# Moving the start of the split U tiles within 128 bytes of memory, step by step and stream by stream

## The reference

```
L0: xw = h @ W1.T;  m = Be * (H.T @ xw);  out = Dn * (H @ m) + b      (twice, hidden width 512)
L1: agg = norm(adj) @ (h @ W);  out = tanh(agg + b)
L2: out = A @ x @ w,  A = exp(leaky(8 tanh(s/8))) * adj^T rescaled by row sums
L3: three times adj @ (x @ W) + b, relu between them
```

## Time and profile before

| | |
|---|---|
| median of 3 runs | 1412.08 us (1411.73 to 1412.53) |
| the profiled execution | 1411.93 us |
| its span, first to last instruction | 1410.1 us |
| PE busy | 1373.2 us, 97% |
| PEld busy | 1324.9 us, 94% |
| DVE, ACT, POOL busy | 87%, 70%, 71% |
| chain that ended last | 95% PE |
| granted TensorE clock, mean | 0.995 |

### The profile page before, as it was taken

The page is one execution under the profiler, slowest core; times in us unless marked ns, Lnnn a source line. Parts: engine busy times, 40 slices in busy tenths (PEclk is TensorE's granted clock), DMA queues, the critical chain, the costliest instruction groups (busy, mean ns, idle before and its releaser), DMA issues.

```text
span 1410.1 us, 34586 instructions
## 1 busy us (share of the span) xinstructions
PE 1373.2 (97%) x10900; PEld 1324.9 (94%) x10900; DVE 1227.0 (87%) x3873; ACT 981.3 (70%) x2312; POOL 997.7 (71%) x2005
## 2 busy tenths in 40 slices
PE   4899999999999999999999999999999999999997
PEld 3799999999999999999999999999999999999996
DVE  5788898898898898898898898898898898898884
ACT  3577777777776777777776777776777777777763
POOL 3677777777777777777777777777777777777751
PEclk8999999999999999999999999999999999999999
DMA  6011121111111111111111111111111111111100
GB/s 190 2 42 36 46 52 34 44 52 34 45 52 34 45 52 34 45 52 33 45 52 32 46 52 31 47 52 31 47 52 30 48 52 29 49 52 31 33 20 23
DMA packets 83079, 62.70 MB, mean 44 GB/s; under 512 B 40304, under 2 KB 65520, under 8 KB 83056
## 3 DMA queue, kind: packets, MB, share of 16 engines
q1 hardware_dynamic: 83056, 62.43, 16.2%
HBM read 45.62 MB, written 16.78 MB: 44 GB/s over the span
## 4 chain that ended last, share of the span: by engine, by line
PE 95%; DVE 2%; POOL 1%; ACT 1%; issue 0%; DMA 0%; SPq 0%; DVEq 0%; POOLq 0%
PE BANK L366 29%; PE BANK L331 24%; PE BANK L373 15%; PE WIDE L366 8%; PE WIDE L342 8%; PE WIDE L373 4%; PE BANK L358 2%; PE BANK L316 2%; PE BANK L385 2%; DMA W<-in_w1t 0%; PE WIDE L279 0%; DVE BN_A L551 0%; POOL LN_A L730 0%; DVE WLO1W L501 0%; DVE BN_C L551 0%
## 5 line engine op out<-in xcount | busy, mean ns | idle before, releaser
L445 ACT ACTIVATE UHI_B<-BANK 128x512 fp32r<-128x512 f32 x96 | 57.2, 596 | 44.8 <-PE BANK L331 44.8
L592 DVE TENSOR_TENSOR ULO_D<-BANK,UHI_D 128x512 fp32r<-128x512 f32 x96 | 66.0, 687 | 24.3 <-ACT UHI_D L445 23.6
L445 ACT ACTIVATE UHI_C<-BANK 128x512 fp32r<-128x512 f32 x96 | 57.2, 596 | 42.1 <-PE BANK L331 42.1
L445 ACT ACTIVATE UHI_D<-BANK 128x512 fp32r<-128x512 f32 x96 | 57.2, 596 | 40.9 <-PE BANK L331 40.9
L445 ACT ACTIVATE UHI_A<-BANK 128x512 fp32r<-128x512 f32 x96 | 57.2, 596 | 40.2 <-PE BANK L331 40.2
L592 DVE TENSOR_TENSOR ULO_C<-BANK,UHI_C 128x512 fp32r<-128x512 f32 x96 | 65.9, 687 | 19.4 <-ACT UHI_C L445 18.7
L592 DVE TENSOR_TENSOR ULO_A<-BANK,UHI_A 128x512 fp32r<-128x512 f32 x96 | 66.0, 687 | 16.1 <-ACT UHI_A L445 15.7
L592 DVE TENSOR_TENSOR ULO_B<-BANK,UHI_B 128x512 fp32r<-128x512 f32 x96 | 65.9, 687 | 14.6 <-ACT UHI_B L445 13.9
L480 ACT ACTIVATE BANK<-BANK 128x256 f32<-128x256 f32 x64 | 23.6, 368 | 63.5 <-DVE BANK L648 63.5
L726 POOL TENSOR_TENSOR LN_D<-MV_D,EPS 128x2 f32<-128x2 f32 x80 | 15.6, 195 | 63.7 <-DVE MV_D L559 63.7
L726 POOL TENSOR_TENSOR LN_A<-MV_A,EPS 128x2 f32<-128x2 f32 x80 | 15.7, 196 | 60.4 <-DVE MV_A L559 60.4
(11 more groups left out here) (501 smaller groups left out, 5940.7 us busy)
## 6 DMA issues: line engine op xcount, KB each, us to landing
X_A<-in_xs SPq DMA_DIRECT2D x16, 256.0 KB, 2.9
X_B<-in_xs SPq DMA_DIRECT2D x16, 256.0 KB, 2.8
X_C<-in_xs SPq DMA_DIRECT2D x16, 256.0 KB, 2.8
X_D<-in_xs SPq DMA_DIRECT2D x16, 256.0 KB, 2.9
out_rows<-O_A SPq DMA_DIRECT2D x16, 256.0 KB, 2.0
out_rows<-O_B SPq DMA_DIRECT2D x16, 256.0 KB, 2.1
out_rows<-O_C SPq DMA_DIRECT2D x16, 256.0 KB, 2.1
out_rows<-O_D SPq DMA_DIRECT2D x16, 256.0 KB, 2.1
```

Of the source, the lines that this page charges most:

```text
L445: nc.scalar.activation(UHI[s][:, 0:J * D], bank(s, step)[:, :], ACT.Copy).then_inc(sem(f"c{step}"), 1)
L592: nc.vector.tensor_tensor(ULO[s][:, 0:J * D], bank(s, step)[:, :], UHI[s][:, 0:J * D].bitcast(F32), ALU.subtract).then_inc(sem(f"l{step}"), 1)
```

## The change

UHI and ULO get 32 more elements (128 bytes) of room each, and a function `u_part` gives the part that a step uses: it begins at element (STARTS + 16) mod 32 of the tile, with one number in STARTS for each pair of steps and stream. Every writer and reader of a step uses the same part: the ACT copy, the DVE subtraction and the matmuls. Since the tiles begin at byte 64, which is 16 elements, the part begins at element STARTS of the 32 that make 128 bytes: at 0 for 0W in all streams, and for 1W to 6W at 24 different places. The number, order, shape and waits of the instructions stay as they are, and tiles behind U move by a multiple of 128 bytes.

```diff
-        UHI = per_stream("UHI", J * DH, dt=F32R)
-        ULO = per_stream("ULO", J * DH, dt=F32R)
+        UHI_ALL = per_stream("UHI", J * DH + 32, dt=F32R)
+        ULO_ALL = per_stream("ULO", J * DH + 32, dt=F32R)
+
+        STARTS = {"0": (0, 0, 0, 0), "1": (6, 18, 20, 26), "2": (4, 22, 30, 13), "3": (2, 10, 24, 12), "4": (8, 14, 17, 28),
+                  "5": (1, 19, 9, 16), "6": (3, 5, 23, 31)}
+
+        def u_part(tiles, step, s):
+            at = (STARTS[step[0]][STREAMS.index(s)] + 16) % 32
+            return tiles[s][:, at:at + J * DH]
...
-                                nc.tensor.matmul(dst, UHI[s][:, at[m]:at[m] + P], w[:, m, :],
+                                nc.tensor.matmul(dst, u_part(UHI_ALL, step, s)[:, at[m]:at[m] + P], w[:, m, :],
...
-                            last = nc.tensor.matmul(dst, ULO[s][:, at[m]:at[m] + P], hi[:, m, :], start=False,
+                            last = nc.tensor.matmul(dst, u_part(ULO_ALL, step, s)[:, at[m]:at[m] + P], hi[:, m, :], start=False,
...
-                    nc.scalar.activation(UHI[s][:, 0:J * D], bank(s, step)[:, :], ACT.Copy).then_inc(sem(f"c{step}"), 1)
+                    nc.scalar.activation(u_part(UHI_ALL, step, s)[:, 0:J * D], bank(s, step)[:, :], ACT.Copy).then_inc(sem(f"c{step}"), 1)
...
-                    nc.vector.tensor_tensor(ULO[s][:, 0:J * D], bank(s, step)[:, :], UHI[s][:, 0:J * D].bitcast(F32),
+                    nc.vector.tensor_tensor(u_part(ULO_ALL, step, s)[:, 0:J * D], bank(s, step)[:, :], u_part(UHI_ALL, step, s)[:, 0:J * D].bitcast(F32),
                                             ALU.subtract).then_inc(sem(f"l{step}"), 1)
```

More of the change, by code:

```diff
@@ L450, in take_hidden @@
                     act.wait_ge(sem("p1U"), c["v"][j])
-                    nc.scalar.activation(UHI[s][:, j * DH:(j + 1) * DH], bank(s, "1U")[:, j, :], ACT.Copy).then_inc(sem("c1U"), 1)
+                    nc.scalar.activation(u_part(UHI_ALL, "1U", s)[:, j * DH:(j + 1) * DH], bank(s, "1U")[:, j, :], ACT.Copy).then_inc(sem("c1U"), 1)
             def hidden_relu(s, c, k):
@@ L599, in low_hidden @@
                     half = slice(j * DH, (j + 1) * DH)
-                    nc.vector.tensor_tensor(ULO[s][:, half], bank(s, "1U")[:, j, :], UHI[s][:, half].bitcast(F32),
+                    nc.vector.tensor_tensor(u_part(ULO_ALL, "1U", s)[:, half], bank(s, "1U")[:, j, :], u_part(UHI_ALL, "1U", s)[:, half].bitcast(F32),
                                             ALU.subtract).then_inc(sem("l1U"), 1)
```

## The result

| | before | after |
|---|---|---|
| median of 5 runs each | 1412.13 us (1411.73 to 1412.53) | 1419.66 us (1419.28 to 1419.67) |
| span of the profiled execution | 1410.1 us | 1417.9 us |

The change costs 7.5 us: the ratio is 1.0052, with a 95% interval of 1.0041 to 1.0063. Forecast were 1406 us; the time lies inside of the range, on the other side of no change. Later kernels ran on several chips, where the kernel before has medians of 1412.1 to 1413.7 us, so the ratio given with each is to the kernel before on its own chip. One execution of e4_place22_everywhere took 1720.67 us at a mean granted clock of 0.752, where its others have 0.994 to 0.996, and is left out.

The account below looks back on a forecast made before the run. PE, busy for 1373.2 of 1410.1 us, was taken to set the pace. The sum 1411.93 - 3.7 (256-column matmuls) - 2.3 (0W) = 1405.9 gave a forecast of 1406 us, range 1391 to 1421.

Parts of the forecast that it names:

- What bounds the kernel: Whole kernel: PE's pace sets the end; DVE, next, has 8.8 us to spare per pass, so PE's savings come out in full.
- Two rhythms of weight load and moving stream: F32R matmuls on PE: weight load and moving stream meet in memory in one of two rhythms, 4.5 ns apart.
- (a): 256-column matmuls of 1W to 6W: half of 52 long turn short, half of 26 short turn long; 3.7 us less.
- (b): 0W, U moved from byte 64 to byte 0: 3 ns per matmul, 2.3 us less; sign: below 394 in all streams.
- (c): The two bias matmuls: only the load beside them changes; 0.4 us at most either way, taken as nothing.
- (d): ACT copy and DVE subtraction at other places: no price, staying near 596 and 687 ns; any cost hidden.
- (e): U steps: untouched and indifferent to the moving operand's place, 275 ns with G at byte 0, 274 at byte 32.
- Rival 1: U's place in all steps: the place does nothing; 1412.1 us, chance 0.20.
- Rival 2: All moved steps: the table hits the short pace everywhere, 20.0 us less, 1392 us; chance 0.11.
- Rival 3: Weight loads of unaligned U cover 33 stretches of 16 bytes, not 32; short steps turn long, 1420 us; chance 0.29.
- The third level: Durations by tile of 256-column matmuls: a level below 276 or above 281 ns would make the forecast wrong; no price given.
- the forecast's own range: Whole kernel: 1399 to 1410 us, with (a) between 0 and 8 and (b) between 0 and 4.6.

Follow-up runs that it names:

- e4_place22_everywhere: U at element 22 of 32 relative to the weights in every step and stream, tiles 4096 bytes apart; 1405.2 us, ratio 0.9939 to the kernel before.
- e7: The change done for 0W alone, all other U at byte 64 with the room of the change; 1412.08 us, ratio 0.9993 to the kernel before.
- p2_kinds: Kernel before plus 18 PE-only series at places 16, 22, 0: unchanged 117.8, 114.5, 118.6 ns; stationary operand repeated 113.5, moving repeated 111.7.
- e2: U at place 0 relative to the weights in every step and stream, tiles 4096 bytes apart; 1421.2 us, ratio 1.0054 to the kernel before.
- p1_all_places: Kernel before plus PE-only series of 16 F32R matmuls at each of 32 places of U; 1529.4 us; only places 10, 19, 22 settle at 113 to 114 ns.
- e1: Changed kernel with U kept at byte 64 everywhere, leaving only the 128 bytes of room; 1412.45 us, ratio 0.9991 to the kernel before.
- p4: Kernel before plus 16 PE-only series, places 16 and 22 moved on by 0 to 7 times 128 bytes; place 22: 113.7 or 113.8 ns at even multiples, 120.0 at odd.

## Why the prediction was wrong, point by point

- **What bounds the kernel** was right for a loss: PE has no idle time after either, and the 123 ns of "all", 64 times, are 7.9 us of the span's 7.8. For a gain it was wrong. "No wait in the middle of the run is left that could grow" rested on busy shares, and 2U's wait for H grew by up to 54 ns as soon as the W steps before it got short (e7: all of a gain of 3.2 us; e4: 20 of 130 ns). The prediction had no term for that wait.
- **Two rhythms of weight load and moving stream** was right as a mechanism (p2_kinds: without one of the two walks, no effect of the place), but the number two was not. The series and e2 show cycles with means of 116.7, 117.8, 118.7 and 120.0 ns, and after has distances up to 126. And the rhythm hangs on the relative address modulo 256 bytes, where the prediction and the change reckoned modulo 128.
- **(a) failed, in the even draw, and with it the sign of the forecast.** I let half of the 26 short matmuls turn long and half of the 52 long ones short. In fact nearly all of the 26 turned long: the share near 113 fell from 0.29 to 0.03, and 2W, 3W and 4W lost 121 ns for each stream and pass, where all 26 x 4.5 = 117 would be the whole. Of the 52 nearly none turned short: 1W, 5W and 6W lost 19 ns. Of the rows of WHI1W, WHI5W and WHI6W, for some of which 276 was the sign, none has a median below 279. The draw isn't even, since 113 is there at 3 of 32 places (p1_all_places), and all three stand in the table for stream B, whose tiles the room moves by an odd multiple of 128 bytes, where none of them is short. Two levels at one place were no reason to take each for as likely at another. The term's upper end of +7.5 us was passed: (121 + 19) x 64 = 9.0, the excess being levels above 118, which the 1 us that I had added for them in the range did not quite cover.
- **(b) was right in sign and near in size:** 0W won 26 ns for each stream and pass, 1.7 us against 2.3. 15 of the 26 came with the room alone, however (e1: 2835), so the place itself gave 11 to 13 ns (after and e7 against e1). The sign that was named for it, below 394 in all four streams, came in part: stream C has medians of 395 and 396.
- **(c) was right:** BIAS4W has 392 ns for 388 and takes 6 ns more of PE's time, 6 x 64 = 0.4 us.
- **(d) was right:** 597 and 686 ns. **(e)** the U steps keep their time in after (2U 891 for 889); in kernels with shorter W steps 2U doesn't, by its wait.
- **Rival 1** (nothing) falls: kernels with the same instructions lie between 1405 and 1421 us.
- **Rival 2** had the possible gain right in its direction, but place 22, at 0.65 near 113, brings 7 us by the ledger (113 x 64 = 7.2) and not 20.
- **Rival 3** gave 1420 and the kernel has 1419.7, yet for the wrong reason. The amount followed from "all 26 fall", which is nearly true (7.7 us for 7.5); that it let 0W gain nothing (1.7 us) and 1W, 5W and 6W lose nothing (1.2 us) cancelled by luck. The cause, one stretch of 16 bytes more, is refuted by place 0 (aligned, 1421.2 us) and place 22 (not aligned, 1405.2 us). The rule of the Trainium skill that stood beside it ("SBUF — State Buffer", Specifications) finds no sign here of a price for the crossing.
- **Not seen at all** was that the 128 bytes of room shift the tiles. I took "a multiple of 128 bytes" for no change. It is worth nothing in sum (e1), but 6 ns for a matmul at place 22 (p4), and it took away the three short places of the table.
- **The third level**, named as what would make the forecast wrong, appeared.
- **A slip in the sums:** the forecast's own range was put at 1399 to 1410 us. With its terms, (a) between 0 and 8 and (b) between 0 and 4.6, it reaches up to 1412.

What stays open: the rule that leads from relative address and moment of entry to a rhythm. I can measure which places have the short one; why 10, 19 and 22, and 13 moved on by 128 bytes, have it wasn't found, nor what in the entry lets 16 settle at 113 in one setting and at 118 in another. Open is as well what sets the moment at which H is ready for 2U: the chain through DVE, POOL and ACT wasn't taken apart.

## What to carry to other kernels

Where PE is never idle and its matmuls are about as long as the load of the next weights, the relative address of the two operands (modulo 256 bytes at least) is a tuning knob of some per cent for each matmul. Don't draw it at random or vary it step by step: measure the places in a series behind the work, take one that settles short after most of what can go ahead (place 22 did after seven of eight), use it for all steps, and check the levels by tile in the whole kernel, since gains of single steps don't add. Where PE has no idle time, look too at how far ahead of each PE step its input is ready: that slack, here nearly 60 ns at 2U, bounds what a faster PE gives, and no busy share shows it. And a tile that grows moves all those behind it; keep such room at multiples of 256 bytes or more if levels are to be compared.

## What the runs showed of the hardware

An F32R matmul of 256 columns behind another starts 111.7 ns later if its moving operand is one repeated element, 113.5 ns later if the stationary one is, and 113 to 123 ns later on average, mostly in repeating cycles, if both walk through memory (113.3 at place 22; 122 at place 27 in p1, 123.3 in 5W of stream B of after). Which of these it is hangs on the relative address of the two modulo 256 bytes and on what ran before. The same cycle of five distances (115, 117, 122, 120, 119) came back for operands both at byte 0, both at byte 64, in the kernel and in the series behind it. With 512 columns the distance is 232 to 233 ns in the series, so the effect of the three places is below 1 ns there on average; in the kernels 0W takes 2822 to 2856 ns, 2.8 ns for a matmul from end to end. With 128 columns it is 111.7 ns for half of the columns, no less than the shortest with 256, so that something else than the columns sets the pace, probably the load. The 32-bit form leaves two rows for a matmul, 215.8 ns each with 256 columns, at each of three places.
